# Seven of eight groups of layer 2's norm computed among layer 1's last slots

## What is computed

```python
def _layernorm(x, axis=-1, eps=1e-05):
    m = jnp.mean(x, axis=axis, keepdims=True)
    v = jnp.var(x, axis=axis, keepdims=True)
    return (x - m) / jnp.sqrt(v + eps)
...
xn = _layernorm(x)                      # layer 1's, then
x = x + L1_attn(xn) * silu(L1_ffn(xn))  # recurrence; attention over masked heads
xn = _layernorm(x)                      # layer 2's norm: the one that moves
x = x + L2_attn(xn) * silu(L2_ffn(xn))  # q = xn @ wq @ fcq_w + fcq_b, ...; top-2 of 8 experts by xn @ Wg
```

## Time and profile before

| | us |
|---|---|
| three runs | 2973.28, 2955.91, 2965.61 |
| their median | 2965.61 |
| the profiled execution, its own time | 2950.37 |
| its span | 2948.6 |
| PE busy in it | 2664.4 (90%) |
| DVE, ACT, POOL busy | 1932.9, 1337.5, 1238.5 |

### The profile page before, as it was taken

How to read it: one execution, slowest core, us unless ns; L and a number is a source line. 1 busy time by engine, 2 the same in 40 slices (tenths; PEclk the granted TensorE clock), 3 DMA queues, 4 the chain that set the end, 5 groups by cost and what they waited for, 6 DMA issues and landing times.

```text
span 2948.6 us, 40534 instructions
## 1 busy us (share of the span) xinstructions
PE 2664.4 (90%) x14378; PEld 1710.1 (58%) x14378; DVE 1932.9 (66%) x3806; ACT 1337.5 (45%) x3436; POOL 1238.5 (42%) x1116
## 2 busy tenths in 40 slices
PE   6799699999999999978999999999987988888988
PEld 3465245555555555553556666665556876766767
DVE  5778666777768777654787777776666172746623
ACT  4455424334343343333556666665452223555533
POOL 2543066667667676761572333320000431333331
PEclk8899799999999999987999999999987786999988
DMA  4453300000000000008412222211002222212113
GB/s 165 135 178 119 105 1 1 1 1 1 1 1 1 1 1 1 1 1 222 99 60 64 67 67 66 66 53 38 22 33 72 66 75 50 62 32 64 41 39 95
DMA packets 172521, 159.55 MB, mean 54 GB/s; under 512 B 98737, under 2 KB 149169, under 8 KB 171505
## 3 DMA queue, kind: packets, MB, share of 16 engines
q1 hardware_dynamic: 149536, 90.92, 11.0%
q0 software_dynamic: 22784, 66.05, 7.1%
HBM read 127.16 MB, written 59.51 MB: 63 GB/s over the span
## 4 chain that ended last, share of the span: by engine, by line
PE 43%; DVE 6%; ACT 4%; issue 1%; SPq 0%; DMA 0%; POOL 0%; DVEq 0%; ACTq 0%
PE bank L65 38%; PE bank L2033 4%; DVE work L3046 0%; ACT weights_odd L2915 0%; ACT L3476 0%; ACT L3216 0%; SPq L3055 0%; DVE work L1989 0%; DVE weights_odd L3307 0%; DVE weights_odd L3305 0%; PE bank L2863 0%; DVE work L3456 0%; DVE work L3257 0%; PE bank L668 0%; DVE work L3305 0%
## 5 line engine op out<-in xcount | busy, mean ns | idle before, releaser
L1491 POOL TENSOR_TENSOR work<-work 128x512 f32<-128x512 f32 x384 | 494.4, 1288 | 318.8 <-DVE work L1483 301.4
L65 PE MATMUL bank<-work 64*128 64x256 f32 (+5 forms) x4384 | 588.5, 352 | 26.8 <-DVE work L3425 9.7
L65 PE MATMUL bank<-weights_odd,normed_channels 128*128 128x512 f32 (+3 forms) x1152 | 524.5, 563 | 24.2 <-DVE work L1483 17.4
L65 PEld LDWEIGHTS bank<-work 64*128 64x128 f32 (+4 forms) x4384 | 411.0, 171 | 216.4 <-issue 130.2
L1483 DVE TENSOR_TENSOR work<-bank,work 128x512 f32<-128x512 f32 x360 | 245.3, 685 | 110.1 <-PE bank L65 106.6
L2003 ACT ACTIVATE work<-bank,work 128x256 f32<-128x256 f32 x512 | 235.5, 472 | 151.0 <-DVE work L1989 151.0
L65 PEld LDWEIGHTS bank<-weights_odd,normed_channels 128*128 128x128 f32 x1152 | 185.2, 197 | 161.4 <-issue 79.7
L595 POOL DMA_INDIRECT weights_even<-in_L_Wx,expert_slots x112 | 112.6, 1005 | 346.3 <-PE bank L668 259.3
L1989 DVE TENSOR_REDUCE work<-bank 128x2 f32<-128x512 f32 x256 | 164.7, 685 | 142.3 <-PE bank L65 142.1
L1558 ACT ACTIVATE work<-bank,work 128x256 f32<-128x256 f32 x256 | 118.9, 470 | 275.2 <-DVE work L1545 275.2
L65 PE MATMUL bank<-work,weights_odd 128*128 128x512 f32 (+3 forms) x520 | 204.4, 509 | 36.0 <-ACT work L3226 16.8
(11 more groups left out here) (344 smaller groups left out, 4627.5 us busy)
## 6 DMA issues: line engine op xcount, KB each, us to landing
filter_matrices<-in_L_filters SPq DMA_DIRECT2D x24, 512.0 KB, 8.4
work<-filter_matrices SPq DMA_DIRECT2D x16, 768.0 KB, 4.3
weights_even<-noted_rows SPq DMA_DIRECT2D x56, 132.0 KB, 2.8
noted_rows<-in_empty SPq DMA_DIRECT2D x11, 660.0 KB, 10.4
noted_rows_in<-in_empty SPq DMA_DIRECT2D x8, 660.0 KB, 10.1
weights_odd<-noted_rows_in SPq DMA_DIRECT2D x40, 132.0 KB, 2.2
work<-token_rows SPq DMA_DIRECT2D x16, 256.0 KB, 3.2
token_rows_out<-in_zeros SPq DMA_DIRECT2D x6, 640.0 KB, 20.5
```

What stands on the lines that cost most here:

```text
L65: return pe.matmul(out, lhsT, rhs, start=first, stop=last, skip_group_check=True)
L1491: gp.tensor_tensor(self.sum_of(p), self.sum_of(p), self.product_of(p), ALU.add).then_inc(s["l1_add"], 1)
```

## The change

Layer 1 gets a reference to layer 2's `Norm` and runs it for groups 0 to 6 in its own slots 488 to 541. They use one of layer 1's two product banks for centering, the other for variance, and the three `prod` buffers for squares. Group g's centering product and Square stand in slot 488 + 8g, its variance product with Ln and Exp four slots later, DVE's multiplication one more slot later. Since all seven groups share one centering bank, group g's centering product waits for group g - 1's multiplication (`ln_done`). Group 7 stays in layer 2. `tensor_joint` moves to banks 2, 3, 4 and 6 and is now held by the seventh multiplication instead of the last residual; the logits go to bank 5, so the first projection waits for the joint weights instead of for DVE's copy of the logits. No arithmetic is added or left out.

```diff
+    def lend(self, groups, cent, var, squares):
+        self.early, self.lent_cent, self.lent_var, self.lent_sq = groups, cent, var, squares
+    def tensor_center(self, pe, on, g):
+        k, s, cent = self.k, self.k.sem, self.places(g)[0]
...
+        on.wait_ge(s["residual"], self.base - GROUPS + g + 1 if g < self.early else self.base)
+        on.wait_ge(s["ln_done"], self.base + (g if g <= self.early else max(self.early, g - len(self.cent) + 1)))
+        mm(pe, cent[:, :], k.center_w, cols(k.xT, g)).then_inc(s["ln_cent"], 1)
+    def tensor_mean(self, pe, on, g):
+        k, s, (_, var, sq) = self.k, self.k.sem, self.places(g)
+        on.wait_ge(s["ln_sq"], self.base + g + 1)
+        on.wait_ge(s["ln_rstd"], 2 * (self.base + g) - 1)
+        mm(pe, var[:, :], k.mean_w, sq).then_inc(s["ln_var"], 1)
+    def scalar_root(self, a, on, g):
+        k, s, (_, var, sq) = self.k, self.k.sem, self.places(g)
+        on.wait_ge(s["ln_var"], self.base + g + 1)
+        a.activation(sq, var[:, :], ACT.Ln, bias=k.eps_ln).then_inc(s["ln_rstd"], 1)
+        on.wait_ge(s["ln_rstd"], 2 * (self.base + g) + 1)
+        a.activation(sq, sq, ACT.Exp, scale=-0.5).then_inc(s["ln_rstd"], 1)
+    def tensor_early(self, pe, on, step):
+        g, half = divmod(step, 2)
+        if 0 <= g < self.early:
+            (self.tensor_center, self.tensor_mean)[half](pe, on, g)
...
     def tensor(self, pe, on, beside=iter(()), logits=None):
...
-        on.wait_ge(s["residual"], base)
+        if self.early == 0:
+            on.wait_ge(s["residual"], self.base)
+        on.wait_ge(s["ln_done"], self.base + self.early)
         for step in range(GROUPS + 3):
-            if step < GROUPS:
...
+            if self.early <= step < GROUPS:
+                self.tensor_center(pe, on, step)
             next(beside, None)
-            if 0 <= step - 1 < GROUPS:
...
+            if self.early <= step - 1 < GROUPS:
+                self.tensor_mean(pe, on, step - 1)
             if logits is not None and step >= 3:
                 logits(pe, on, step - 3)
...
+    NORM = 488
+    def lend(self, norm):
+        self.next_norm = norm
+        norm.lend(GROUPS - 1, self.b_prod[0], self.b_prod[1], self.prod)
+    def norm_step(self, slot):
+        step, rest = divmod(slot - self.NORM, 4)
+        return step if self.next_norm is not None and rest == 0 and step >= 0 else None
...
+            if (n := self.norm_step(slot)) is not None:
+                on.wait_ge(self.k.sem["l1_prod"], L1_UNITS * BATCH)
+                self.next_norm.tensor_early(pe, on, n)
+            if (n := self.norm_step(slot)) is not None:
+                on.wait_ge(s["l1_add"], 4 * L1_UNITS * BATCH // L1_E)
+                self.next_norm.scalar_early(a, on, n)
+            if (n := self.norm_step(slot - 1)) is not None:
+                self.next_norm.vector_early(v, on, n)
...
-        self.norm = Norm(k, n, self.p[0:3], k.bank[0:4])
+        self.norm = Norm(k, n, self.p[0:3], (k.bank[0], k.bank[1], k.bank[7]))
+        self.b_joint = (b[2], b[3], b[4], b[6])
-        self.router = Router(k, n, nth, self.Wg, self.b_misc, work, k.route_steps)
+        self.router = Router(k, n, nth, self.Wg, self.b_o, work, k.route_steps)
...
-        self.shared_free = (s["route"], self.router.at + 1)
+        self.shared_free = (s["l2_joint"], self.JOINT)
```

More of the change, by code:

```diff
@@ new lines, in scalar_square @@
+    def scalar_square(self, a, on, g):
+        s, (cent, _, sq) = self.k.sem, self.places(g)
+        on.wait_ge(s["ln_cent"], self.base + g + 1)
+        on.wait_ge(s["ln_done"], self.base + g - 2)
+        a.activation(sq, cent[:, :], ACT.Square).then_inc(s["ln_sq"], 1)
+    def scalar_root(self, a, on, g):
[4 more added lines that the diff above has]
+        a.activation(sq, sq, ACT.Exp, scale=-0.5).then_inc(s["ln_rstd"], 1)
@@ L1880, in tensor_joint @@
     def tensor_joint(self, pe, on):
-        s, b = self.k.sem, self.k.bank[4:8]
+        s, b = self.k.sem, self.b_joint
         on.wait_ge(s["l2_small"], self.SMALL)
@@ L2051, in tensor_times_v @@
         g, m, b = self.unit(n)
+        on.wait_ge(s["route"], self.router.at + 1)
         self.wait_turned_scores(on, 2 * n)
@@ L3784, in build @@
             stages.append((Layer0, Layer1, Layer2, Layer3)[which](k, n, nth))
+        for stage, following in zip(stages, stages[1:]):
+            if isinstance(stage, Layer1):
+                stage.lend(following.norm)
         def tensor_program(pe):
```

65 lines of the change are left out of this document (34 added, 31 removed).

## The result

| | before | after |
|---|---|---|
| median, us | 2960.76 | 2982.81 |
| lowest to highest of four runs | 2951.68 to 2973.28 | 2980.83 to 2985.80 |
| the profiled execution, its own time | 2950.37 | 2980.83 |
| its span | 2948.6 | 2979.0 |

The changed kernel is slower by 0.8%: ratio **1.0081, 95% interval 1.0057 to 1.0104**, 22.05 us by the medians. The time lies inside the range (2959 to 2992) and past the forecast of 2976.6, in the case "slower by over 0.5%" to which the prediction gave 0.32.

The account below looks back on a forecast made before the run. Layer 2's body is bound by PE, so the logits copy's time decides: residual +28.4 us, less 16.0 back, is +12.4 cold (+5.4 warm), taken as +11 on the median 2965.61: 2976.6 us, range 2959 to 2992.

Parts of the forecast that it names:

- slower by over 0.5%: Whole program: rivals 1 and 4 and the forecast's upper edge with the spread of the runs; chance 0.32.
- The path: Layer 1's last residual to layer 2's copy of the logits: the result is the change of that copy's time.
- The relay and the first half: Layer 1's attention, groups 0 to 2: a group's chain from centering to multiplication takes 6.4 us warm, 8.3 cold; outputs +12.7 us.
- the walk: The new order of layer 1's slots followed forward with profiled durations; in the first half, scaled outputs at 1327.1 instead of 1314.42.
- The second half: Layer 1 behind the scaled outputs, groups 3 to 6: adds 15.7 us, so the last residual comes 28.4 us later.
- the cold variant of the sum: Whole program with products of the second half at 1.2 GHz: +28.4 - 16.0 = +12.4 us.
- +11: Whole program: value chosen between +12.4 us (second half at 1.2 GHz) and +5.4 (2.4 GHz throughout), nearer the cold one.
- What layer 2 gives back: Layer 2's start, last residual to copy of the logits: 13.7 instead of 29.6 us, 16.0 us back.
- rival 1: Layer 1's slots colder or more tightly blocked: +15 to +25 us, 2981 to 2991; chance 0.26.
- Rival 2: Layer 1's waits take relay and roots, only the last insertion delays: -13.8 us, 2951.8; chance 0.13 with half-way cases.
- Rival 3: Layer 1's roots need fewer table loads, Exp's gone: 1.3 us less per group, +2 us, 2968; chance 0.03.
- Rival 4: Each table load in layer 1's slots costs a second 1.3 us beyond its row: +24 us, 2990; chance 0.01.

Follow-up runs that it names:

- idle products in the second half: Changed kernel plus unread centering products, three behind each variance product of groups 3 to 5, two ahead of layer 2's joint products: ratio to before 1.0026.
- one set and wide products: Changed kernel with one load of the set for Ln and Exp, and an unread 128x512 product behind logits of groups 0 to 5: ratio to before 1.0017.

## Why the prediction was right or wrong

**The path.** Right. Layer 2's body kept its length, and what reached the copy late made the program late by about the same: +23.13 us at the copy, +22.05 by the medians, with the 4 us of doubt in the first number.

**The relay and the first half.** Right. 8.34 us cold against 8.3; a group every 8.3 to 11.8 us against 8 to 12; scores 4/5 +4.0 against +4.3; outputs +14.8 against +12.7. The 2.1 us more aren't mainly in the roots (for group 0 the walk had counted Ln's load): root 2 ended 31.5 us behind head 0's transposes, against 31.0 in the walk. From there to the end of the last product with v the walk had 4.2 us and the trace has 5.8, for the row of PE from 1321.62 to 1326.44 holds a projection that waits for ACT's copies (L1705), centering 3 at 1.2 GHz (2.07) and that product at 1.2 GHz (1.81, where before it took 1.10). All of it is less than the 4.2 us by which this stretch varied with unchanged code, so the match in the first half is in part luck.

**The second half.** Right: 15.84 us against 15.7, at 1.2 GHz, as the cold variant of the sum had it. The "+11", a value between cold and warm, was a choice away from what came: the cold sum of the prediction was +12.4.

**What layer 2 gives back.** This step failed. The prediction let residual to copy shrink by 16.0 us, to about 14; it shrank by 7.54, to 22.78. The order and the handovers were right; the durations of PE's products were not. It costed layer 2's start from rows of before at 2.4 GHz (logits 0.85 a group, centering 1.1), since there that stretch had been at 1.00. But the change takes the wide products out of that stretch and leaves a row of narrow ones behind a second half at 1.2 GHz. Measured, the logits of four groups took 3.6 us more than reckoned, and from centering 7 to the copy it was 10.49 us instead of 6.5. The two together are 7.6 us of the miss of 8.5; the rest lies in the two joint products for v ahead of the logits (3.78 us, 1.98 in the run that came to them warm). The prediction named 20 us as the bound from which this step would be wrong, and it was passed. It had asked which clock the second half would have, and not what clock the stretch behind it would start with and keep. How much of the 8.5 us is the clock itself was not measured apart: the run that came to the logits at 2.4 GHz won only 3.7 of it back, and moving six groups of logits away won 12.2.

**The forecast against its rivals.** The number that came is that of rival 1 (+15 to +25), which had 0.26. Its size was right and its reason only in part: the relay wasn't blocked more tightly, and the first half didn't fall to 1.2 GHz (granted clock 0.70, 0.86 and 0.94). The cold place was one that no rival named. Rival 2 (the relay fits) is refuted by every wait of DVE for the root, 3.1 to 6.6 us. Its point of decision, 5.2 to 6.8 us for eight slots, was a good one: with one table set the relay took 6.1 to 9.5, the residual came 15.6 us late instead of 30.7, and the ratio was 1.0008, though the local sum was still 5.8 us above before's 72.70. Rival 3 (fewer loads) didn't come by itself: 14 loads stand in the trace. Put in by hand, it was worth 17.4 us locally, where the rival reckoned 9.1: it took out six of the Ln loads too, and the clock stood higher. The Trainium skill (ScalarE: Activation LUTs, Table sets: the hidden batching unit) says that Ln followed by Exp needs one load. Here that holds only where the kernel names the set itself. Rival 4 (about 2.7 us a load) is refuted: 1.28 us and 0.01 to 0.02 to the function.

**The clock.** What the traces show: a stretch with PE busy 4.00 of 4 us at 0.50 for 20 us (after), the fall from 1.00 to 0.50 in a row of 128x8 products (idle products in the second half), and a return to 1.00 when wide products were put between them (one set and wide products). In before, 128x8 products between wide ones ran at 1.00. So the clock that a stretch gets isn't told by its busy time in the records alone. DMA traffic isn't it either: the row of before at 1.00 has 293 GB/s, the one of after at 0.50 has 329, and the one at 1.00 in one set and wide products has 317. The rows of 128x8 products are the suspect for the clock staying down; no run measured them by themselves. For the fall itself PE's waits ahead of the joint products are a rival that no run excludes: 1.25 and 1.57 us in the run with idle products, 1.30 and 1.57 in the one with wide products, in which the clock fell in its joint products, before the first 128x8 product. The Trainium skill (TensorE: Matmul & The Clock Gate, What's actually happening) says that the clock follows how busy PE has been of late. By the busy time of the records alone this stretch would have run at 2.4 GHz, and by an estimate (23.1 less 7.6) the sum would have been nearer to +15 than +23; the measurement decides.

**Still open.** How the 17.4 us of the loads divide; why kernels with the same code in the attention get the higher clock at different times, which is worth 4 us; what made the clock fall in the joint products of the run with wide products and not in those of the run with idle products; and the 10 us behind the copy, which lie within what copy to end varies by.

## What to carry to other kernels

Work moved into another stage's waits is a relay there: sum its steps, and compare that with what the slots leave, before counting what it saves; if the sum is larger, it sets the pace and everything queued behind it is late. Before moving functions of two kinds into a stretch, make sure of the table set that serves both, for a load between two steps of a relay is paid by everything behind it. Before reading a gain of a few microseconds off one profile, look at how far two profiles of unchanged code lie apart. And ask what the old place looks like once the wide products are gone: what is left may run at half the clock.

## What the runs showed of the hardware

- PE at granted clock 0.50 for 20 us without a gap in its records, in a stretch mostly of 128x8 products; 8 of them in a group took 1.71 us, where 8 among wide products at 1.00 took 0.95.
- A table load is issued ahead of its function's wait, so it hides only if ACT is idle before the data come; 14 loads alone (17.9 us) cost 4 to 8 us, and 13 in a relay (16.6 us) gave 17.4 back when taken out, the clock's part in it.
- One PSUM bank less for centering (three to two) lengthened an eight-group norm from 30.3 to 49.6 us, about 7 us of the 19.3 waiting, the rest longer products at a lower granted clock (0.64 against 1.00).
- Idle products of 128x512 in PE's waits shortened the path by 9.2 us where the relays held 14 loads and by 2.5 us where they held one, both at 1.2 GHz for the most part.
- The same code of layer 1 took 42.38 us in one profile and 46.67 and 46.59 in two others, with the granted clock over 1300 to 1304 at 1.00 in the first and at 0.50 in the others.
